# Second norm's statistics by bn_stats on VectorE instead of squares on ScalarE, with new step lists for all engines

## What is computed

```python
h = layer_norm(x, ln1_g, ln1_b); hx = token_shift(h)
k, v = mix(h, hx, tm_mix_k) @ wk, mix(h, hx, tm_mix_v) @ wv
r = sigmoid(mix(h, hx, tm_mix_r) @ wr)
x = x + (r * wkv_scan(k, v, time_decay, time_first)) @ wo
h = layer_norm(x, ln2_g, ln2_b); hx = token_shift(h)
kk = square(relu(mix(h, hx, cm_mix_k) @ cwk))
x = x + sigmoid(mix(h, hx, cm_mix_r) @ cwr) * (kk @ cwv)
```

## Time and profile before

| | |
|---|---|
| median of 3 runs | 734.31 us |
| profiled execution | 735.36 us |
| its span, first to last instruction | 733.5 us |
| PE matmul busy | 695.9 us (95%), 3797 |
| DVE busy | 590.6 us (81%), 1003 |
| ACT busy | 554.7 us (76%), 1086 |
| POOL busy | 137.2 us (19%), 220 |
| chain that ended last | PE 74%, DVE 5%, issue 2%, ACT 2% |

### The profile page before, as it was taken

One profiled execution on the slowest core, in us unless ns is written; L12 is line 12 of the kernel. 1 busy time (PEld: TensorE's weight loads), 2 busy tenths in 40 slices (PEclk: granted clock), 3 DMA queues, 4 the chain that ended last, 5 costly groups with the idle time before them and its releaser, 6 DMA issues.

```text
span 733.5 us, 11006 instructions
## 1 busy us (share of the span) xinstructions
PE 695.9 (95%) x3797; PEld 591.1 (81%) x3797; DVE 590.6 (81%) x1003; ACT 554.7 (76%) x1086; POOL 137.2 (19%) x220
## 2 busy tenths in 40 slices
PE   6888799999999999999999999999999999799877
PEld 5858667788799978997898869897898879698767
DVE  0878757889887879889788889788888889794796
ACT  2584899898869986798769986798679877772431
POOL 2301320521032301421043202320052001200100
PEclk9999999999999999999999999999999999899999
DMA  5710010100010000101010100101010000000000
GB/s 162 230 30 29 0 30 1 29 1 29 1 57 2 29 2 15 43 1 30 15 44 1 29 1 16 44 1 29 15 44 2 0 1 15 16 0 15 15 1 29
DMA packets 13394, 19.40 MB, mean 26 GB/s; under 512 B 998, under 2 KB 10780, under 8 KB 13340
## 3 DMA queue, kind: packets, MB, share of 16 engines
q1 hardware_dynamic: 10736, 10.31, 4.3%
q0 software_dynamic: 2560, 8.39, 3.9%
q10 hardware_dynamic: 44, 0.01, 0.0%
HBM read 14.51 MB, written 4.19 MB: 25 GB/s over the span
## 4 chain that ended last, share of the span: by engine, by line
PE 74%; DVE 5%; issue 2%; ACT 2%; ACTq 0%; DVEq 0%
PE psB L603 19%; PE psC L678 14%; PE psB L632 11%; PE psC L706 9%; PE psA L594 8%; PE psA L564 5%; PE psC L693 3%; PE psA L551 1%; PE psB L574 1%; PE psC L662 1%; PE psA L574 1%; DVE scales L1228 1%; ACT normc L939 1%; DVE normc L1243 0%; DVE normc L1246 0%
## 5 line engine op out<-in xcount | busy, mean ns | idle before, releaser
L603 PE MATMUL psB<-cwv_s,kkT 128*128 128x256 f32 x512 | 113.1, 379 | 0.7 <-ACT kkT L922 0.7
L603 PEld LDWEIGHTS psB<-cwv_s,kkT 128*128 128x128 f32 x512 | 96.6, 190 | 16.3 <-issue 2.9
L678 PE MATMUL psC<-up_hi,xq_hi 128*128 128x352 f32 x256 | 86.5, 338 | 6.6 <-DVE xq_lo L1341 4.0
L594 PE MATMUL psA<-mix,kvr_s 128*128 128x512 f32 x192 | 86.4, 594 | 2.4 <-DVE mix L1055 1.3
L678 PE MATMUL psC<-up_lo,xq_hi 128*128 128x352 f32 x256 | 83.4, 326 | 0.0
L678 PE MATMUL psC<-up_hi,xq_lo 128*128 128x352 f32 x256 | 83.3, 326 | 0.0
L594 PEld LDWEIGHTS psA<-mix,kvr_s 128*128 128x128 f32 x192 | 35.6, 190 | 38.9 <-issue 36.2
L462 POOL TENSOR_SCALAR sc_c<-sc_c 128x2 f32<-128x2 f32 x16 | 8.3, 521 | 295.2 <-DVE h L1208 295.0
L1055 DVE SCALAR_TENSOR_TENSOR mix<-hT,rest,mix 128x512 f32<-128x512 f32 x80 | 54.3, 743 | 7.9 <-ACT mix L836 7.9
L632 PE MATMUL psB<-key_hi,cwk_hi 128*128 128x512 f32 x128 | 57.5, 449 | 0.6 <-DVE key_lo L1191 0.6
L564 PE MATMUL psA<-w_s,rowsT 128*128 128x256 f32 x256 | 58.0, 379 | 0.0
(11 more groups left out here) (188 smaller groups left out, 1740.5 us busy)
## 6 DMA issues: line engine op xcount, KB each, us to landing
out<-h SPq DMA_DIRECT2D x16, 256.0 KB, 2.1
mix<-L_attn_cwk SPq DMA_DIRECT2D x1, 1024.0 KB, 7.6
cwv_s<-L_attn_cwv SPq DMA_DIRECT2D x1, 1024.0 KB, 9.2
hq<-L_ffn_w_gate SPq DMA_DIRECT2D x1, 704.0 KB, 5.8
hq<-L_ffn_w_up SPq DMA_DIRECT2D x1, 704.0 KB, 7.8
w_s<-L_tok_w SPq DMA_DIRECT2D x1, 512.0 KB, 3.5
rows<-L_tok_w,ids_now POOLq DMA_INDIRECT x30, 4.1
h<-L_ffn_w_down SPq DMA_DIRECT2D x1, 352.0 KB, 7.4
```

Of the source, the lines that this page charges most:

```text
L594: mm = nc.tensor.matmul(psA[:, A.slot(f"{name}{d}")], kvr_s[:, w, k, d * P:(d + 1) * P], mix[:, w, k].rearrange("p c t -> p (c t)"), start ...
L603: mm = nc.tensor.matmul(psB[:, B.slot(name), q * D:(q + 1) * D], lhsT(k, 2 * j + q), weight[:, k, :], start=(k == 0), stop=(k == nk - 1))
L678: mm = nc.tensor.matmul(psC[:, C.slot(name), f, 0:INTER // 2], a[:, k, t * P:(t + 1) * P], b[:, w, k, f * (INTER // 2):(f + 1) * (INTER // ...
```

## The change

`b_x1` adds y with two plain additions of 128 x 512 in place of four of 128 x 256 with row sums. DVE then takes `bn_stats` of each of the four tiles and `bn_aggr` of each result, which gives mean and variance (`mv_b`). `b_dev` on ACT and `b_mean` on POOL go away. `b_coef` on POOL is four instructions in place of three. The first and the third norm keep their statistics on ACT. The lists of all engines and the table `WARM` are new. Where the lists differ for the first chunks, written out by `walk` (step.chunk):

The diff, lists in full, the rest without its context lines:

```diff
 ORDER = {
-    "pe": [("c_up3", 2), ("a_k", 0), ("b_key2", 1), ("a_v", 0), ("b_key3", 1), ("c_down0", 2), ("a_r", 0),
-        ("w_turn2", 1), ("b_value0", 1), ("c_turn2", 2), ("c_turn3", 2), ("w_par", -1), ("b_value1", 1),
-        ("a_turn0", -1), ("c_down1", 2), ("b_out0", 0), ("b_out1", 0), ("c_cols0", 1), ("a_emb0", -1),
-        ("c_up0", 1), ("c_cols1", 1), ("a_turn1", -1), ("b_cols", 0), ("a_emb1", -1), ("w_turn0", -1),
-        ("c_up1", 1), ("b_gate", 0), ("c_turn0", 1), ("b_key0", 0), ("c_up2", 1), ("a_cols", -1), ("w_turn1", 0),
-        ("c_turn1", 1), ("b_key1", 0)],
-    "act": [("c_turn1", 2), ("w_par", -3), ("a_part", 0), ("c_sq2", 2), ("b_key1", 1), ("a_k", 0), ("w_turn1", 1),
-        ("c_up3", 2), ("b_key2", 1), ("w_turn0", 0), ("a_wkv1", 0), ("a_v", 0), ("a_wkv2", 0), ("c_sq3", 2),
-        ("b_key3", 1), ("w_turn2", 1), ("a_wkv3", 0), ("c_dev0", 1), ("a_r", 0), ("c_turn2", 2), ("c_turn3", 2),
-        ("c_norm0", 1), ("a_y", 0), ("a_turn0", -1), ("c_sqn0", 1), ("c_dev1", 1), ("c_cols0", 1), ("c_norm1", 1),
-        ("b_dev", 0), ("a_emb0", -1), ("w_sq2", 0), ("c_sqn1", 1), ("c_up0", 1), ("b_norm", 0), ("a_turn1", -1),
+    "pe": [("c_up3", 2), ("a_k", 0), ("b_key2", 1), ("a_v", 0), ("w_turn2", 1), ("b_key3", 1), ("a_r", 0),
+        ("c_down0", 2), ("b_value0", 1), ("w_par", -1), ("c_turn2", 2), ("c_turn3", 2), ("b_value1", 1),
+        ("a_turn0", -1), ("b_out0", 0), ("c_down1", 2), ("b_out1", 0), ("c_cols0", 1), ("a_emb0", -1),
+        ("c_up0", 1), ("a_turn1", -1), ("b_cols", 0), ("c_cols1", 1), ("a_emb1", -1), ("c_up1", 1), ("b_gate", 0),
+        ("c_turn0", 1), ("b_key0", 0), ("a_cols", -1), ("w_turn0", -1), ("c_up2", 1), ("c_turn1", 1),
+        ("b_key1", 0), ("w_turn1", 0)],
+    "act": [("b_key0", 1), ("a_cols", 0), ("c_turn1", 2), ("c_sq2", 2), ("a_part", 0), ("b_key1", 1), ("a_k", 0),
+        ("w_turn1", 1), ("b_key2", 1), ("c_up3", 2), ("a_wkv1", 0), ("a_v", 0), ("a_wkv2", 0), ("b_key3", 1),
+        ("c_sq3", 2), ("w_turn2", 1), ("a_wkv3", 0), ("c_dev0", 1), ("a_r", 0), ("c_turn2", 2), ("c_turn3", 2),
+        ("w_par", -4), ("c_norm0", 1), ("a_y", 0), ("c_sqn0", 1), ("c_dev1", 1), ("a_turn0", -1), ("c_cols0", 1),
+        ("c_norm1", 1), ("a_emb0", -1), ("c_up0", 1), ("c_sqn1", 1), ("b_norm", 0), ("w_sq2", 0), ("a_turn1", -1),
         ("b_cols", 0), ("c_cols1", 1), ("b_part", 0), ("a_emb1", -1), ("c_sq0", 1), ("w_sq0", -1), ("a_dev", -1),
-        ("b_high", 0), ("c_up1", 1), ("b_gate", 0), ("c_turn0", 1), ("a_norm", -1), ("c_sq1", 1), ("c_up2", 1),
-        ("w_sq1", -1), ("b_key0", 0), ("w_key", -1), ("a_cols", -1)],
-    "dve": [("c_rq2", 2), ("a_wkv1", 0), ("w_split1", 1), ("c_up3", 2), ("c_sq3", 2), ("a_wkv2", 0), ("a_wkv3", 0),
-        ("c_down0", 2), ("w_low", 1), ("c_rq3", 2), ("b_value0", 1), ("w_key", 0), ("a_wkv4", 0), ("c_low2", 2),
-        ("c_low3", 2), ("c_sn0", 1), ("b_value1", 1), ("w_split0", 0), ("c_rn0", 1), ("c_down1", 2), ("b_x1", 0),
-        ("c_split0", 1), ("c_sn1", 1), ("c_rn1", 1), ("w_par", -8), ("w_quant2", 0), ("c_up0", 1), ("c_sq0", 1),
-        ("c_split1", 1), ("b_mix", 0), ("w_quant0", -6), ("c_rq0", 1), ("b_low", 0), ("c_up1", 1), ("c_sq1", 1),
-        ("c_low0", 1), ("c_rq1", 1), ("c_up2", 1), ("c_sq2", 1), ("w_quant1", -5), ("c_low1", 1), ("a_mix", -1)],
-    "pool": [("b_sum", 1), ("b_coef", 1), ("a_mean", 0), ("a_coef", 0), ("gather0", -1), ("c_mean0", 1),
-        ("c_coef0", 1), ("gather1", -1), ("c_mean1", 1), ("c_coef1", 1), ("b_mean", 0)],
-    "sp": [("c_down0", -4), ("c_down1", -4)],
+        ("b_high", 0), ("c_up1", 1), ("w_key", -1), ("b_gate", 0), ("a_norm", -1), ("w_sq1", -1), ("c_turn0", 1),
+        ("c_sq1", 1), ("w_turn0", -1), ("c_up2", 1)],
+    "dve": [("a_wkv1", 0), ("c_up3", 2), ("w_split1", 1), ("c_sq3", 2), ("a_wkv2", 0), ("a_wkv3", 0),
+        ("w_quant1", -4), ("w_key", 0), ("w_low", 1), ("c_down0", 2), ("c_rq3", 2), ("b_value0", 1), ("a_wkv4", 0),
+        ("c_low2", 2), ("c_low3", 2), ("c_sn0", 1), ("b_value1", 1), ("c_rn0", 1), ("c_down1", 2), ("w_par", -8),
+        ("b_x1", 0), ("w_quant2", 0), ("c_split0", 1), ("c_sn1", 1), ("c_rn1", 1), ("c_up0", 1), ("c_sq0", 1),
+        ("c_split1", 1), ("b_mix", 0), ("c_rq0", 1), ("b_low", 0), ("c_up1", 1), ("c_sq1", 1), ("w_quant0", -7),
+        ("c_low0", 1), ("c_rq1", 1), ("w_split0", 0), ("c_up2", 1), ("c_sq2", 1), ("c_low1", 1), ("a_mix", -1),
+        ("c_rq2", 1)],
+    "pool": [("c_coef1", 2), ("b_sum", 1), ("b_coef", 1), ("a_mean", 0), ("a_coef", 0), ("gather0", -1),
+        ("c_mean0", 1), ("c_coef0", 1), ("gather1", -1), ("c_mean1", 1)],
+    "sp": [("c_down1", -3), ("c_down0", -4)],
 }
 
 
-WARM = {("w_par", 0): 10, ("a_turn0", 0): 14, ("w_turn0", 0): 72, ("a_k", 0): 54, ("a_r", 0): 12, ("a_turn0", 1): 96,
-        ("b_out0", 0): 8, ("b_cols", 0): 18, ("c_turn3", 7): 20}
+WARM = {("w_par", 0): 10, ("a_turn0", 0): 14, ("w_turn0", 0): 90, ("a_k", 0): 42, ("a_r", 0): 12, ("a_turn0", 1): 96,
+        ("b_out0", 0): 8, ("b_cols", 0): 16, ("c_up0", 6): 18, ("c_up0", 7): 10, ("c_cols1", 7): 8, ("c_turn3", 7): 20}
...
-        sc_b = sb("sc_b", [P, 6, TILES])
+        sc_b = sb("sc_b", [P, 4, TILES])
+        mv_b = sb("mv_b", [P, TILES, 2])
+        stat = sb("stat", [P, TILES, 6])
...
-        a_mean, b_mean, c_mean = signal("a_mean", 1), signal("b_mean", 1), signal("c_mean", 2)
-        a_spread, b_spread, c_spread = signal("a_spread", TILES), signal("b_spread", TILES), signal("c_spread", TILES)
-        a_coef, b_coef, c_coef = signal("a_coef", 6), signal("b_coef", 3), signal("c_coef", 6)
+        a_mean, c_mean = signal("a_mean", 1), signal("c_mean", 2)
+        a_spread, b_stat, c_spread = signal("a_spread", TILES), signal("b_stat", 2 * TILES), signal("c_spread", TILES)
+        a_coef, b_coef, c_coef = signal("a_coef", 6), signal("b_coef", 4), signal("c_coef", 6)
...
-            def mean_b(ch):
-                B.wait_emptied(pool, ch, "o1")
-                mean(sc_b, b_mean)
-
-                hold(pool, b_spread, ch, TILES)
-                coefficients(ch, sc_b, b_coef)
+                hold(pool, b_stat, ch, 2 * TILES)
+                nc.gpsimd.tensor_scalar(sc_b[:, 0], mv_b[:, :, 1], EPS, None, ALU.add).then_inc(b_coef.sem, 1)
+                nc.gpsimd.tensor_scalar(sc_b[:, 2], mv_b[:, :, 0], -1.0, None, ALU.mult).then_inc(b_coef.sem, 1)
+                at(pool, b_coef, ch, 1)
+                nc.gpsimd.tensor_tensor(sc_b[:, 1], sc_b[:, 0], power[:].to_broadcast([P, TILES]), ALU.pow).then_inc(b_coef.sem, 1)
+                at(pool, b_coef, ch, 3)
+                nc.gpsimd.tensor_tensor(sc_b[:, 3], sc_b[:, 2], sc_b[:, 1], ALU.mult).then_inc(b_coef.sem, 1)
...
-            walk("pool", {"gather0": gather(0), "gather1": gather(1), "a_mean": mean_a, "b_mean": mean_b, "c_mean0": mean_c(0), "c_mean1": mean_c(1),
+            walk("pool", {"gather0": gather(0), "gather1": gather(1), "a_mean": mean_a, "c_mean0": mean_c(0), "c_mean1": mean_c(1),
...
-            def dev_b(ch):
-                at(act, b_mean, ch, 1)
-                at(act, b_fin, ch.back(1), 2)
-                for t in range(TILES):
-                    spread(rr[:, t, :], x1[:, t, :], sc_b, t, b_spread)
-
...
-                at(act, b_coef, ch, 3)
+                at(act, b_coef, ch, 4)
...
-            walk("act", {**each(turn_a, "a_turn", 2), **each(emb, "a_emb", 2), "a_dev": dev_a, "b_dev": dev_b, **each(dev_c, "c_dev", 2),
+            walk("act", {**each(turn_a, "a_turn", 2), **each(emb, "a_emb", 2), "a_dev": dev_a, **each(dev_c, "c_dev", 2),
...
-                    for q in range(2):
-                        t = 2 * j + q
-                        i = nc.vector.scalar_tensor_tensor(out=x1[:, t, :], in0=psB[:, B.slot(f"o{j}"), q * D:(q + 1) * D],
-                                                           scalar=1.0, in1=y[:, t, :], op0=ALU.mult, op1=ALU.add,
-                                                           accum_out=sc_b[:, 4, t:t + 1])
-                    i.then_inc(b_dve.sem, 1)
+                    nc.vector.tensor_tensor(x1[:, 2 * j:2 * j + 2, :].rearrange("p t d -> p (t d)"), psB[:, B.slot(f"o{j}")],
+                                            y[:, 2 * j:2 * j + 2, :].rearrange("p t d -> p (t d)"), ALU.add
+                                            ).then_inc(b_dve.sem, 1)
+                B.wait_emptied(dve, ch, "o1")
+                for t in range(TILES):
+                    nc.vector.bn_stats(stat[:, t, :], x1[:, t, :]).then_inc(b_stat.sem, 1)
+                for t in range(TILES):
+                    hold(dve, b_stat, ch, t + 1)
+                    nc.vector.bn_aggr(mv_b[:, t, :], stat[:, t, :]).then_inc(b_stat.sem, 1)
```

## The result

The changed kernel takes **749.21 us** (median of 4 runs, 748.27 to 749.75) against 734.35 us for the kernel before: a ratio of 1.0195, 95% interval 1.0174 to 1.0216. It is slower by 14.9 us. The forecast was 749.3 us.

What follows compares the result with a forecast made beforehand. PE bounds the middle; at both ends a chain of single steps through ACT, DVE and POOL does. 11.3 + 1.5 + 3.0 - 1.4 + 0.6 = 15.0 us on the profiled 735.36, less 1.05 to the median: 749.3 us, range 742 to 757.

Steps and rivals of the forecast that it cites:

- The start: Fill: 90 warm-ups and w_turn0 behind a_cols on PE delay a_k from 40.17 to 51.5 us, +11.3 us.
- slow clock of 2.0 us: Fill: after about 11 us idle PE starts slow, adding 2.0 us to a_cols and the transposes behind it.
- The rival of the free start: Fill: the 90 transposes don't hold ACT or are covered, only 3.7 us of other terms stay: 738.0; chance 8%.
- The statistics on DVE: Second norm, each chunk: the new DVE statistics add 1.9 us behind the last x1, bounds 1.7 and 3.4.
- Chunk 0: Chunk 0: b_mix on DVE comes about 1.9 us later, partly absorbed on ACT: +1.5 us, bounds 0 and 3.
- The middle: Six middle periods: c_cols1 behind b_cols leaves PE's wait one filler less, 0.5 us each: +3.0 us, bounds 0 and 7.
- DVE becomes the bound: Rival, each chunk: DVE's 1.3 to 2.8 us more before xq_lo stall c_up0, giving 756.5; chance 12%.
- The sentence on GpSimd: Second norm: bn_stats has one input, so by the shared-interface rule POOL's add doesn't lengthen it.
- The last full period: Drain: 18 warm-ups ahead of c_up0, less slow clock and b_norm about 1 us sooner: -1.4 us, bounds -2.9 and 0.
- the last chunk: Drain: c_up0 ahead of c_sqn1 on ACT makes DVE wait one activation more: +0.6 us, bounds 0 and 0.7.
- The sum: Whole kernel: 11.3 + 1.5 + 3.0 - 1.4 + 0.6 = 15.0 us, forecast 749.3 us.

Runs made afterwards that it cites:

- e3: The changed kernel with a_cols of chunk 0 ahead of w_turn0 on ACT alone, PE's list and warm-ups unchanged: 751.46 us, ratio 1.022 to the kernel before.
- e8: The kernel before with 18 warm-up transposes ahead of c_up0 of chunk 6 and nothing else: 735.23 us, ratio 0.9994.
- e10: The kernel before with two exchanges on PE alone, a_r ahead of c_down0 and b_out0 ahead of c_down1: 735.26 us, ratio 0.9998.
- e12: The kernel before with its remaining PE pauses of 1.2 to 2.2 us filled by warm-up transposes, no other edit: 733.79 us, ratio 0.998.
- e9: The changed kernel with the start's order of before and w_sq2 ahead of c_up0, c_sqn1 and b_norm on ACT: 738.16 us, ratio 1.0034 to the kernel before.
- e4: The kernel before with the second norm's statistics on VectorE alone, its lists without b_dev and b_mean: 737.21 us, ratio 1.0025.
- e7: The changed kernel with c_sqn1 ahead of c_up0 on ACT and c_cols1 ahead of a_turn1 and b_cols on PE: 749.04 us, ratio 1.0173 to the kernel before.
- e5: The changed kernel with the four bn_stats of each chunk run twice on VectorE: 753.96 us, ratio 1.0243 to the kernel before.
- e6: The changed kernel with c_sqn1 ahead of c_up0 on ACT again, the rest as it is: 751.01 us, ratio 1.0209 to the kernel before.
- e11: The kernel before with the statistics on VectorE alone and 24 warm-up transposes ahead of c_up0 of chunk 6: 736.84 us, ratio 1.0018.

## Why the prediction came out right

**The start (+11.3, measured 11.16 in the profile and 11.3 between medians).** The step held in its numbers: the forecast had the 106 transposes end at 46.1 us and PE ended them at about 46.2, ACT's casts at 46 (46.24), hT at 47.6 (47.52), a_k at 51.5 (51.33). Its slow clock of 2.0 us measured 0.9 in a_cols and 1.9 in the 90, 2.8 together, offset by a_cols starting 0.66 earlier. One sentence of it held only just: that the 42 warm-ups ahead of a_k end before a_k is ready. They end 0.21 us before it, so PE's chain alone gives nearly the same start (e3). The rival of the free start (738.0) gives just the time of a kernel whose start is put back (737.87). The 2.0 us were read off as lost clock in windows of 20 us (1.8 and 3.2 us), and that isn't lost time: against e8, e10 and e12 these two places cost the kernel before some 0.8 and 0.6 to 0.8 us, as the slow clock there fell partly on work that something else held. At the start nothing hid it, and its price was 2.8.

The page "TensorE: Matmul & The Clock Gate" of the Trainium skill (Part 1) calls the throttled clock the default, released by activity. The traces agree: the first a_cols behind the pause of 10.83 us takes 1.97 us instead of 1.09, and the granted clock is back at 1.00 in the window from 40 us, before the 90 end.

**The statistics on DVE (1.9 us, measured 1.7).** The timeline of DVE in chunk 0, whose forms answer to those of the earlier trace rows:

```profile
84.47 0.69 DVE L1173 TENSOR_TENSOR mix<-psB,takev 128x512 f32<-128x512 f32 x1 [0.94 <-PE psB L607]
85.20 1.41 DVE L1178 BATCH_NORM_STATS2 stat<-mix 128x6 f32<-128x256 f32 x4
86.52 0.41 DVE L1181 BATCH_NORM_AGGREGATE mv_b<-stat 128x2 f32<-128x6 f32 x4
```

Bounding bn_stats by the 256-wide rows (0.34 to 0.42 each) and bn_aggr by the small accumulator read was good: 0.33 from start to start, and about 0.1.

**Chunk 0 (+1.5, measured 0.9).** The mechanism was right in its first half: b_mix and with it b_gate come 1.76 us later behind a_k (forecast: about 1.9). But only 0.77 of that reach the key products, which before had waited 0.64 us for key_lo behind b_gate and now wait for nothing. The timelines of ACT and DVE:

```profile
90.21 2.08 ACT L888 ACTIVATE mix<-mix,sc_b 128x256 f32<-128x256 f32 x4 [1.21 <-POOL sc_b L510]
92.19 0.78 ACT L980 ACTIVATE xq_hi<-h 128x704 fp32r<-128x704 f32 x1
```

```profile
93.07 0.89 DVE L381 SCALAR_TENSOR_TENSOR h<-xq_hi,h 128x704 f32<-128x704 f32 x1 [2.16 <-ACT xq_hi L980]
```

w_quant2 on DVE waits 2.16 us for w_sq2, which now comes behind b_norm, and b_mix waits for w_quant2. Putting w_sq2 back takes 1.0 us of b_mix's delay away (e9), and the statistics by themselves make the stretch to the key products 0.6 us longer (e4 beside e8, e10 and e12). That they don't make it 1.7 longer has a reason for which the prediction had no term. DVE's two scalings of w_quant2, before and after:

```profile
75.47 1.34 DVE L370 TENSOR_SCALAR scales<-scales 128x44 f32<-128x44 f32 x2
```

```profile
88.45 0.31 DVE L373 TENSOR_SCALAR scales<-scales 128x44 f32<-128x44 f32 x2
```

In the kernel before they run beside POOL's add of 128 x 1024 (from 74.28 to 76.67 us). One such TENSOR_SCALAR of each chunk meets that add there and takes 0.67 to 1.25 us, where those that don't take 0.19. In the changed kernel the statistics stand beside the add, and no TENSOR_SCALAR does. So DVE gets part of the time back.

**The middle (+3.0 for six periods, measured 1.17 for five, 0.23 each, so 1.4).** This is the term that was mis-sized. The wait is as forecast: 1.06 us ahead of b_cols, and the distance from c_up0 to b_cols is 6.11 us in both kernels, since ACT's chain sets it.

```profile
323.69 1.06 PE L578 MATMUL psB<-ident,mix 128*128 128x128 f32 x8 [1.06 <-issue]
324.59 0.60 PE L666 MATMUL psC<-ident,normc 128*128 128x128 f32 x4
```

But the filler that moved behind it is 0.44 us from start to start, not 0.5, and about 0.2 us of it come back in the rest of the period, where PE waits for nothing. Which exchange gives them wasn't found: e10 tried two and saw none. And the cause was told in half: with the statistics on DVE the filler would have been late ahead of b_cols too (e7), and the statistics alone, with the old lists, lengthen a period by 0.14 to 0.21 of the 0.23 us (e4). The fear that DVE becomes the bound had a real basis: xq_lo ends at 317.15 and c_up0 starts at 317.58, so 0.43 us were left, not 0.1. The rival fell as argued, since a stall there comes off the wait ahead of b_cols (e5). The sentence on GpSimd held for bn_stats: 18 of the 32 ran wholly beside its add, for 407 to 411 ns each, and those clear of it took 427 or 428. The page "GPSIMD Engine Reference" of the Trainium skill (its spec table) names as contending VectorE's instructions with two SBUF inputs or in a two-port mode. The trace agrees for bn_stats, but one input alone doesn't spare an instruction, as the TENSOR_SCALAR above shows; whether that one ran in a two-port mode no row tells.

**The last full period (-1.4, measured -1.2) and the last chunk (+0.6, measured +0.7).** The first came out near its size, with a cause that the prediction didn't have. It counted on the slow clock and on b_norm coming 1 us sooner since b_dev is gone. The clock is a part: the kernel before takes 97.0 to 97.2 us for this stretch where its profile has 97.81, the changed one 96.57. But b_norm comes sooner (83.52 us behind c_up0 of chunk 5 instead of 84.37) by an exchange on ACT. Before, then after:

```profile
630.13 0.63 ACT L963 ACTIVATE square<-normc 128x512 fp32r<-128x512 f32 x1 [1.07 <-DVE normc L1234]
630.78 1.28 ACT L955 ACT_TABLE_LOAD   x1
...
632.73 2.06 ACT L890 ACTIVATE mix<-mix,sc_b 128x256 f32<-128x256 f32 x4
```

```profile
640.66 1.28 ACT L953 ACT_TABLE_LOAD   x1
643.93 0.76 ACT L953 ACTIVATE hq<-psC 128x704 f32<-128x704 f32 x1 [1.98 <-PE psC L682]
...
645.10 2.07 ACT L888 ACTIVATE mix<-mix,sc_b 128x256 f32<-128x256 f32 x4
```

The silu of c_up0 needs another table than the steps ahead of it, and the load takes 1.28 us. With c_sqn1 first it stood between c_sqn1 and c_up0, on the chain to b_norm; with c_up0 first it falls into ACT's wait for PE. e6, where c_sqn1 is first again and b_dev is gone all the same, has b_norm at 84.78 us, and the stretch takes 98.01 us there and 97.57 in e7 (both with some slow clock behind it). So b_dev's going brought nothing here, and the exchange did. That and its longer periods fit e6 being slower than the changed kernel. The term of the last chunk is shown by e6 and e7, and by ACT's rows:

```profile
705.88 0.76 ACT L953 ACTIVATE hq<-psC 128x704 f32<-128x704 f32 x1 [2.08 <-PE psC L682]
706.53 0.62 ACT L961 ACTIVATE square<-normc 128x512 fp32r<-128x512 f32 x1
```

**The sum.** By the landmarks 11.16 + 0.89 + 1.17 - 1.24 + 0.74 = 12.72 us; the forecast's sum was 15.0. The medians differ by 14.9. So the total was met better than its terms, and that is luck: the middle was put too high by 1.6 us and chunk 0 by 0.6, and two things outside the prediction made up for it. The median of the four runs of the kernel before lies 0.7 to 1.1 us below its medians beside the experiments. And the pair of profiles is uneven: the first met the slow clock behind two pauses, at 66 and 627 us, for about 1.5 us, and the second is the fastest run of its kernel, with a granted clock of 1.00 from 640 to 660 us, where its near copies e5, e6 and e7 show windows of 5 us at 0.72 to 0.94. Against e12, the kernel before at full clock, the landmarks of the changed kernel sum to 14.86 us: 11.81 up to a_k, 1.56 in chunk 0 up to the key products and 0.09 behind them, 1.37 over five periods, -0.64 and 0.67. Which of the two sets of terms is nearer to a usual execution stays open, as there is one profile of the changed kernel; in both the start is some 80 to 88% of the sum.

## What to carry to other kernels

Warm-up work belongs ahead of the wait that it covers: 90 transposes placed in the list behind the step that ends the pause became 10 us of critical path, on PE's list and, through one exchanged pair, on ACT's too. Before moving statistics to an engine that has slack on average, look at which single hand-over comes next in its list; here 1.2 us more on DVE fitted into the 1.6 us that xq_lo had in the middle, and the hand-over behind it, normc to c_cols1, was the one that came late. Look also at what the freed steps ran beside: an instruction on DVE that met POOL's add, or a table load on ACT that a changed order hides, moved as much as the terms that were costed. And when executions of one kernel spread, or two profiles are compared, set their mean granted clocks beside the times: here an equal span hid a cost of 2 us. Filling PE's pauses of 1 to 2 us with transposes bought 1.3 us, where exchanging two steps on PE bought nothing.

## What the runs showed that I had not expected

A part of the spread of 3 us and more between executions of the same kernel goes with the TensorE clock. Of 74 executions of the kernel before, the 21 at a mean granted clock of 0.998 or more have a median of 734.6 us, and the 40 at 0.995 or less one of 735.7; the rest of the spread isn't explained. Beside e12 the kernel before ran from 733.83 (clock 0.998) to 738.2 us (0.993), and with four pauses filled from 732.94 to 735.24 us, 11 of 12 runs at 0.999 or 1.0. The same pause of 2.03 us was followed by full clock in one execution (e4) and by 0.78 and 0.88 in another (e11), so one profile can't tell what a pause costs on average. And the 90 transposes behind the pause took 11.89 us in one profile and 11.13 in another (e3).
